# A two-layer graph network kernel: loads in another order, statistics inside the load, key and value scaling on ScalarE

## The reference, cut to what matters

```python
xn = _layernorm(x, axis=-1)                                    # per node: mean and variance over 256
# graph part, twice (w11,b11,w12,b12 and w21,b21,w22,b22):
msg = jax.nn.relu(x[src]); agg = segment_sum(msg, dst); h = x + agg
h = relu(h @ w1 + b1);     out = h @ w2 + b2
# mixing part (4 heads of 64):
k = _layer_norm(split(xn @ wk.T), ln_k_g, ln_k_b)              # normalised per head
v = _layer_norm(split(xn @ wv.T), ln_v_g, ln_v_b)
kv = einsum('bhsd,bhse->bhde', k, v) / S                       # sum over all nodes
```

## Time and profile before

| | us |
|---|---|
| median of 3 runs | 4442.27 (4441.02 to 4442.47) |
| the profiled execution | 4439.19 |
| its span, first to last instruction | 4437.5 |
| PE, DVE, POOL, ACT busy | 3168.6, 2979.4, 2691.2, 2177.9 |
| mean granted TensorE clock | 0.846 |

### The profile page before, as it was taken

The page is one execution under the profiler, slowest core; times in us unless marked ns, Lnnn a source line. Parts: engine busy times, 40 slices in busy tenths (PEclk is TensorE's granted clock), DMA queues, the critical chain, the costliest instruction groups (busy, mean ns, idle before and its releaser), DMA issues. The chain is left out here.

```text
span 4437.5 us, 62914 instructions
## 1 busy us (share of the span) xinstructions
PE 3168.6 (71%) x14543; PEld 2333.6 (53%) x14544; DVE 2979.4 (67%) x7344; ACT 2177.9 (49%) x5198; POOL 2691.2 (61%) x2846
## 2 busy tenths in 40 slices
PE   3477777777766666777776947777777774699993
PEld 1255555555544555555555835555555553556662
DVE  5577777777756777777776447777777778734444
ACT  4644444444433333444443437877787876622220
POOL 0477777776747776777774657777777770034441
PEclk9688888888877878888888978999899896699996
DMA  5334443333323333333332221111212131311115
GB/s 159 103 112 115 116 115 110 111 112 109 112 80 107 109 102 101 110 112 108 111 110 69 70 45 36 35 36 35 36 35 35 35 30 27 139 50 62 60 60 192
DMA packets 233965, 378.41 MB, mean 85 GB/s; under 512 B 72570, under 2 KB 157027, under 8 KB 233404
## 3 DMA queue, kind: packets, MB, share of 16 engines
q0 software_dynamic: 120320, 278.00, 24.5%
q1 hardware_dynamic: 100580, 84.26, 5.9%
q10 hardware_dynamic: 12760, 12.80, 0.9%
HBM read 318.43 MB, written 56.42 MB: 84 GB/s over the span
## 5 line engine op out<-in xcount | busy, mean ns | idle before, releaser
L1494 PE MATMUL conv_ps<-conv_msg,conv_S 128*128 128x256 f32 x3328 | 1081.7, 473 | 404.4 <-DVE ACC L1504 319.3
L1494 PEld LDWEIGHTS conv_ps<-conv_msg,conv_S 128*128 128x128 f32 x3328 | 736.5, 235 | 653.0 <-DVE ACC L1504 312.3
L1470 POOL DMA_INDIRECT conv_msg<-conv_table,GI x832 | 794.5, 955 | 327.4 <-issue 248.1
L1470 POOL DMA_INDIRECT conv_msg<-relu_xn_table,GI x832 | 789.1, 948 | 315.9 <-issue 248.7
L1504 DVE TENSOR_TENSOR ACC<-ACC,conv_ps 128x256 f32 x1664 | 700.6, 421 | 410.0 <-issue 251.7
L2339 POOL DMA_INDIRECT gat_msg<-attn_table,GI x832 | 789.7, 949 | 268.6 <-issue 251.3
L1479 ACT ACTIVATE conv_S<-iota_row,LOC 128x128 f32<-128x128 f32 x1664 | 507.4, 387 | 522.2 <-PE conv_ps L1494 506.8
L2399 PE MATMUL gat_ps<-gat_M,gat_S 128*128 128x260 f32 x1664 | 501.1, 435 | 191.1 <-DVE ACC L2457 177.4
L2399 PEld LDWEIGHTS gat_ps<-gat_M,gat_S 128*128 128x128 f32 x1664 | 328.0, 215 | 314.3 <-DVE ACC L2457 245.8
L2457 DVE TENSOR_TENSOR ACC<-ACC,gat_ps 128x260 f32 x832 | 349.1, 420 | 125.2 <-PE gat_ps L2399 102.6
L1525 ACT COPY conv_hs<-ACC 128x256 f32 x98 | 39.6, 404 | 588.0 <-DVE ACC L1504 588.0
(11 more groups left out here) (551 smaller groups left out, 5687.5 us busy)
## 6 DMA issues: line engine op xcount, KB each, us to landing
conv_msg<-relu_xn_table,GI POOLq DMA_INDIRECT x832, 2.8
conv_msg<-conv_table,GI POOLq DMA_INDIRECT x832, 2.8
gat_msg<-attn_table,GI POOLq DMA_INDIRECT x832
combine_y<-answers SPq DMA_DIRECT2D x24, 512.0 KB
relu_xn_table<-begin_rx SPq DMA_DIRECT2D x49, 128.0 KB, 1.7
xnT<-begin_xt SPq DMA_DIRECT2D x49, 128.0 KB, 1.8
conv_kv_xt<-xnT SPq DMA_DIRECT2D x49, 128.0 KB
conv_table<-conv_a SPq DMA_DIRECT2D x49, 128.0 KB
```

What stands on the lines that cost most here:

```text
L1470: pool.indirect_dma_start(self.msg[:, h * RING + k, :], None, table, bass.IndirectOffsetOnAxis(ap=self.m.GI[:, t:t + 1], axis=0)).then_inc ...
L1494: self.nc.tensor.matmul(self.ps[k % self.NB][:, 0:D], self.S[:, r % 2, k, :], self.msg[:, r % self.DEEP * RING + k, :], start=True, stop=T ...
```

## The change

Four things are changed.

1. **Loads.** SP now starts the edges, the four weight matrices, then the features in their five pieces, and then the rest. ACT starts the small transfers. The one semaphore becomes several (`edges_in`, `weights_in`, `x_in[0..4]`, `next_in`, `loaded`), and each engine waits for those it uses.
2. **Statistics.** The 49 `bn_stats` and the chain behind them move from stage begin into stage load, on VectorE, each group of 12 tiles behind its own transfer. The root moves with them. Of the 49 instructions that fill ACC, 22 move from ScalarE to VectorE, behind `off_made`.
3. **Run tables.** The second of the two tables in steps 9 to 16 moves to the even round that follows.
4. **Key and value scaling.** VectorE only takes the reciprocal; ScalarE scales, with eight instructions of 64 columns (`act_norm`), behind the root and ahead of the one-hots of the next round.

```diff
@@ stage_load
+            sp.dma_start(src_i...).then_inc(edges_in, 16)
+            sp.dma_start(dst_i...).then_inc(edges_in, 16)
+            for k, w in enumerate((m.wk, m.wv, m.wo, m.fw)):
+                sp.dma_start(nat[k][:, :, :], chunks(w)).then_inc(weights_in, 16)
+            for g in range(4):
+                sp.dma_start(m.X[:, g * 12 * D:(g + 1) * 12 * D]...).then_inc(x_in[g], 16)
+            sp.wait_ge(x_clear, 1)
+            sp.dma_start(m.X[0:TAIL, (TILES - 1) * D:TILES * D], ...).then_inc(x_in[4], 16)
...
-            pe.wait_ge(loaded, count[0])
+            pe.wait_ge(weights_in, 112)
...
-            for g in range(4):
-                act.dma_start(m.X[:, g * 12 * D:(g + 1) * 12 * D]...).then_inc(x_in, 16)
+            act.dma_start(gWlr[0:4, :], m.gWr).then_inc(weights_in, 16)
+            act.dma_start(gWlr[4:8, :], m.gWl).then_inc(weights_in, 16)
+            act.dma_start(gWs[:, :, :], chunks(m.gW)).then_inc(weights_in, 16)
+            for to, frm, how in small:
+                act.dma_start(to, frm, **how).then_inc(loaded, 16)
...
+            act.wait_ge(var_done, 1)
+            nc.scalar.activation(root[:, :], va[:, :], ACT.Sqrt).then_inc(root_done, 1)
...
-            v.wait_ge(loaded, count[0])
+            v.wait_ge(edges_in, 32)
...
+            for i in range(TILES):
+                if i % 12 == 0:
+                    v.wait_ge(x_in[i // 12], 16)
+                nc.vector.bn_stats(parts[:, i, :], m.X[:, i * D:(i + 1) * D])
+            v.drain()
...
@@ class KeyValueSums
     def dve_norm(self, v, i):
         v.wait_ge(self.rooted, i + 1)
+        nc.vector.reciprocal(self.s2[:, :], self.rt[:, :]).then_inc(self.inverted, 1)
+
+    def act_norm(self, act, i):
+        act.wait_ge(self.inverted, i + 1)
         if i >= 1:
-            v.wait_ge(self.kn_used, i)
-        nc.vector.reciprocal(self.s2[:, :], self.rt[:, :])
-        v.drain()
-        r = self.s2[:, :].unsqueeze(2).broadcast_to([P, 8, 64])
-        nc.vector.tensor_tensor(self.groups(self.kn[:, :]), self.groups(self.pkv[:, 0:D]), r[:, 0:4, :], ALU.mult)
-        for c in range(2):
-            last = nc.vector.tensor_tensor(...)
+            act.wait_ge(self.kn_used, i)
+        for g in range(8):
+            to = self.kn[:, g * 64:g * 64 + 64] if g < 4 else self.vn[:, (g - 4) // 2, g % 2 * 64:g % 2 * 64 + 64]
+            last = self.nc.scalar.activation(to, self.pkv[:, g * 64:g * 64 + 64], ACT.Copy, scale=self.s2[:, g:g + 1])
         last.then_inc(self.kn_made, 1)
@@ stage_begin
-            for i in range(TILES):
-                nc.vector.bn_stats(parts[:, i, :], m.X[:, i * D:(i + 1) * D])
...
             v.drain().then_inc(off_made, 1)
+            for i in range(BY_ACT, TILES):
+                nc.vector.tensor_scalar(m.ACC[:, i * AW:i * AW + D], m.X[:, i * D:(i + 1) * D], m.mean[:, i:i + 1],
+                                        m.rstd[:, i:i + 1], ALU.subtract, ALU.mult)
...
-            for i in range(TILES):
+            for i in range(BY_ACT):
                 nc.scalar.activation(m.ACC[:, i * AW:i * AW + D], ...)
@@ class RunTables
+    def dve_sums_past(self, v, i, k):
+        nc, t = self.nc, (self.frm, self.to)[k]
+        v.drain()
+        nc.vector.tensor_tensor(self.by[:, 0:TILES - 1], t[:, 1:TILES], t[:, 0:TILES - 1], ALU.subtract)
+        ...
+        nc.vector.tensor_reduce(self.at[k][:, RUNS // 8 * (i - 9):RUNS // 8 * (i - 8)], self.picked, X_AXIS, ALU.add)
+        v.drain()
@@ stage_conv1, ScalarE
                     kv.act_root(act, i)
+                    kv.act_norm(act, i)
@@ stage_conv2, VectorE
                     tables.dve_step(v, k)
+                if here(k := turn_of(r, 2, 17)) and k >= 9:
+                    tables.dve_sums_past(v, k, 1)
```

More of the change, by code:

```diff
@@ L194, in _ @@
+        for lo in (0, 64):
+            small += [(m.kgp[lo:lo + 64, :], m.kg.rearrange("(p a) -> p a", a=1), {}),
+                      (m.kbp[lo:lo + 64, :], m.kb.rearrange("(p a) -> p a", a=1), {}),
+                      (m.vgr[:, lo:lo + 64], row_to_all(m.vg), {}), (m.vbr[:, lo:lo + 64], row_to_all(m.vb), {})]
         @block.sync
         def _(sp):
[L196 to L200, removed]
@@ L211, in _ @@
[L211 to L220, removed]
+            sp.dma_start(src_i[:, :], m.src.rearrange("(p c) -> p c", p=LANES)).then_inc(edges_in, 16)
@@ L226, in _ @@
             sp.wait_ge(pads_out, 48)
-            sp.wait_ge(loaded, count[0])
-            sp.wait_ge(x_in, 80)
+            sp.wait_ge(next_in, 16)
+            sp.wait_ge(loaded, len(small) * 16)
         @block.gpsimd
@@ L310, in _ @@
             nc.vector.tensor_tensor(m.packed[:, :], m.packed[:, :], dst_i[:, :], ALU.bitwise_or)
+            for i in range(TILES):
[3 more added lines that the diff above has]
+            v.drain()
+            f = lambda k: parts[:, :, k]
+            nc.vector.tensor_tensor(va[:, :], f(1), f(4), ALU.add)
+            nc.vector.tensor_tensor(vb[:, :], f(1), f(4), ALU.subtract)
+            nc.vector.tensor_tensor(root[:, :], f(2), f(5), ALU.add)
+            v.drain()
+            nc.vector.tensor_scalar(m.mean[:, :], va[:, :], 0.5, None, ALU.mult)
+            nc.vector.scalar_tensor_tensor(out=vb[:, :], in0=vb[:, :], scalar=0.25, in1=vb[:, :], op0=ALU.mult, op1=ALU.mult)
+            v.drain()
+            nc.vector.scalar_tensor_tensor(out=vb[:, :], in0=root[:, :], scalar=1.0 / D, in1=vb[:, :], op0=ALU.mult, op1=ALU.add)
+            v.drain()
+            nc.vector.tensor_scalar(va[:, :], vb[:, :], 1e-5, None, ALU.add)
+            v.drain().then_inc(var_done, 1)
+            v.wait_ge(root_done, 1)
+            nc.vector.reciprocal(m.rstd[:, :], root[:, :])
+            v.drain()
+            nc.vector.scalar_tensor_tensor(out=m.shift[:, :], in0=m.mean[:, :], scalar=-1.0, in1=m.rstd[:, :], op0=ALU.mult, op1=ALU.mult)
 def stage_stats(nc, m, name, eps, with_rms=False):
@@ L831, in stage_begin @@
         wrong, bin_f2 = st.sb("wrong", [LANES, 4]), st.sb("bin_f2", [P, SC])
-        parts = st.sb("parts", [P, TILES, 6])
-        va, vb, shift = (st.sb(n, [P, TILES]) for n in ("va", "vb", "shift"))
-        scaled = st.sem("scaled")
+        va = st.sb("va", [P, TILES])
         xn, rx, xt = (st.sb(n, [P, w, D]) for n, w in (("xn", KEEP), ("rx", 2), ("xt", 2)))
```

88 lines of the change are left out of this document (33 added, 55 removed).

## The result

| | before | after |
|---|---|---|
| median, us (range, runs) | 4441.65 (4439.24 to 4442.47, 4) | 4382.93 (4378.77 to 4384.98, 4) |
| ratio, 95% interval | | 0.9869 [0.9856, 0.9881] |
| profiled execution: own time, span, mean granted clock | 4439.19, 4437.5, 0.846 | 4381.45, 4379.8, 0.857 |

What follows compares the result with a forecast made beforehand. VectorE was taken to bound conv1's cycles, DMA the load. Gains of 23.8 - 0.5 + 38 + 1 = 62.3 us took the profiled 4439.2 to 4376.9; with 3.1 for the median, 4380 us, 8 in 10 within 4364 to 4406.

Steps and rivals of the forecast that it cites:

- Features: Stage load: last features landed at 36 us, so the first one-hot starts at 46.3 instead of 70.09, 23.8 us earlier.
- The worst bound: Stage load: at worst the features take as long as all loads did before, 39.3 us, and the gain is 20.5.
- The 23.8 are kept to its end: Stage begin: from the one-hots on it is the same work in the same order, so the 23.8 us gain stays.
- Fills and gathers: End of stage begin: 22 operations on ACC take 7.3 us, hidden in VectorE's gap of 10.35; 0.5 charged for gathers.
- The rival of starved gathers: End of stage begin: the 22 operations lock GpSimd's gathers out, 7 us less gain, 4387 us; chance 0.05.
- Conv1: Scaling off VectorE takes 0.89 us from each of 46 cycles, 40.9, less 3: 38 us, bounds 0 and 42.
- slow cycles: Conv1: 3 us taken off the gain for cycles in which TensorE runs slowly.
- The room of 0.4: Conv1, fifth addition: with VectorE 0.9 us sooner and TensorE 1.0 later, 0.4 us of room remains.
- The gathers didn't take over: Conv1: rival that GpSimd's gathers bound the cycle, so it doesn't get shorter, 4418 us; chance 0.03; gathers put at 20.0.
- The slow rival: Conv1: TensorE at 1.2 GHz delays the fifth addition, cycle 23.4 us, 4501 if all 46 so; chance of slower 0.04.
- Tables: Conv2 table cycles: split steps cover TensorE's late sum, 1.6 us less 0.6 for drains, 1 us gain; bounds -2 and 3.

Runs made afterwards that it cites:

- e6: The changed kernel with the feature groups alone and first in SyncE's queue, edges, weights and small transfers in ScalarE's: 4381.55 us, 0.9873 of before.
- e11: The changed kernel with the features in eight loads of 6 tiles instead of four of 12: 4376.37 us, 0.9852 of before.
- e5: The changed kernel without SyncE's wait, at the start of stage begin, for the store of the packed edges: 4379.83 us, 0.9867 of before.
- e9: The changed kernel with the store of the packed edges moved from stage begin into the load, behind the features: 4376.94 us, 0.9854 of before.
- e10: The changed kernel with 44 of the 49 fills of ACC on VectorE instead of 22: 4391.04 us, 0.9884 of before.
- e1: The kernel before with the key and value scaling on ScalarE and nothing else: 4395.51 us, 0.9901 of before.
- e7: The changed kernel with twelve scalings for a tile instead of eight, four being cut in two: 4399.25 us, 0.9909 of before.
- e2: The kernel before with the new order of loads, the statistics in the load and the split fill of ACC only: 4421.95 us, 0.9957 of before.
- e8: The changed kernel with ScalarE's square of the projected tile ahead of its copy of the node's row in conv1: 4369.82 us, 0.9844 of before.

## Why the prediction was right

The sum came within 5 us, and that is in part luck: the load gave 5.7 us less than worked out, and conv1 5.7 more.

**Features (predicted: last at 36, begin at 43.7).** Mis-sized. The last full group landed at 39.8, and begin started at 48.12. Behind the landing all went nearly as worked out: 13 tiles in 4.34 (4.3), the chain in 3.1 (2.6), the barrier 0.8. So the landing has 3.8 of the 4.4 us that are missing, and the first one-hot came 19.4 us sooner instead of 23.8. The other orders gave the same: 40.0 with the features first (e6), 39.98 with groups of six (e11). The bytes were nearly right (8.96 MB counted, 9.5 moved by 40 us), the rate wasn't: 320 GB/s was the best 10 us of the earlier trace rows, while the first 40 us ran at a mean of 242 before and 238 after. At 242, start included, 8.96 MB take 37 us. The worst bound, 39.3, was the nearest.

**"The 23.8 are kept to its end".** This step failed, by 1.7 us. I took the statistics for work that covers nothing, but SyncE's store of the edges ran under them. e5 and e9 show that it is the store itself, ahead of the small ones, and only to a small part the wait for it.

**Fills and gathers.** Right, 7.3 us hidden with 3 to spare. The rival of starved gathers didn't come: beside 22 fills their data were used 0.03 us later, and e10, with 44, lost VectorE's own time and at most 0.2 more. The rule behind the rival, in the Trainium skill (SBUF — State Buffer, section "SBUF: two separate sides"), speaks of operations of VectorE in a two-port mode; by their times (e10) the fills seem not to be in it, so the rule is neither confirmed nor refuted here. That the fills would be such operations was the prediction's reading of it. What the traces show beside them is 0.99 against 0.94 for a gather.

**Conv1 (predicted 38, measured 43.7).** The mechanism was right (e1). The cycle fell by 0.94 where 0.89 was worked out, 45 times 42; the 3 us taken off for slow cycles were not lost. Where the other 0.05 of a cycle comes from isn't shown. The scalings took 0.20 each where 0.22 was assumed, the projection 2.13 where 2.2. The room of 0.4 at the fifth addition was 0.3 (e7), and had four more instructions gone into the scaling, 20 us of the 43 would have been lost again. The gathers didn't take over (20.64 against 20.1).

**The slow rival** had its mechanism right, as e7's waits of 2.1 us show, and its odds wrong way round: in the stage the granted clock rose from 0.84 to 0.92. Of the 46 projections before from 240 us on, five took 2.7 to 3.0 us instead of 1.96, so ran partly at the low level; of the 45 after, none took over 2.6.

**Tables (predicted -1, measured +1.0 to +2.5).** A cost where a gain was forecast; 1.5, by the means, lies inside the bounds of -2 and 3 us of gain, on the wrong side. I counted 0.2 us per cycle of TensorE's late sum as saved. In seven table cycles VectorE's waits for TensorE did fall from 8.3 to 3.2 us, but its issue time rose from 24.9 to 30.5: the late sum had lain over time in which VectorE itself would not have been ready. The gaps too short to be put down to anyone rose from 7.4 to 8.3 us, about what the added drains may take (0.6 was assumed).

## What to carry to other kernels

Before a stage's long operation is moved away, list what else ran under it, transfers and their queues above all; a store that nobody waited for becomes the first thing that everybody waits for. Price a stream of loads by its mean rate over the whole load, not by its best stretch, and make the last group small, since all of its tiles stand behind the last landing. When two terms of a sum miss, look whether they miss in opposite directions before the sum is believed. An idle time's releaser is only the last of several: taking it away gives back no more than the next one leaves, so look for the issue time under the wait.

## What was not expected of the hardware

Moving the features ahead of 1.8 MB of other loads brought the first group 5 us forward and the last not at all (40.0). Small stores (128 KB each, 1.7 us to landing as a rule) took until 52.3 when issued at 47 behind a store of 0.4 MB in the same queue; that store, in 125 rows, ran at 82 GB/s with 0.31 of the DMA engines busy. Issuing the four feature loads kept SyncE's queue busy for 26 us, and the engine did nothing else in that time. In conv1, TensorE did the same matmuls in 4% less time (929 instead of 970 us for 45 cycles) at a higher mean granted clock (0.92 instead of 0.84). The rise comes with the scaling on ScalarE (e1 0.91, e2 0.85), but it alone doesn't set the cycle: in e8 the cycle is shorter still, 20.34, at 0.89. Why the clock rose is open. Of seven gathers started by GpSimd beside 44 float32 `tensor_scalar` of VectorE the last four took 0.98 to 0.99 us instead of 0.94, no more.
